# The attention loop's segment mask: made in setup and loaded per group, instead of subtracted by GpSimd

## The reference, cut to what matters

```
edge_dst, edge_src = (edge_index[0], edge_index[1])
...
attn = jnp.einsum('ehd,ehd->eh', q[edge_src], k)
amax = jax.ops.segment_max(attn, edge_src, num_segments=n)
ex = jnp.exp(attn - amax[edge_src])
denom = jax.ops.segment_sum(ex, edge_src, num_segments=n)
alpha = ex / (denom[edge_src] + 1e-16)
upd = jax.ops.segment_sum(v * alpha[..., None], edge_src, num_segments=n)
```

## Time and profile before

| what | us |
|---|---|
| median of 3 runs (5847.3 to 5866.55) | 5865.84 |
| the profiled execution | 5866.98 |
| its span, from the first to the last instruction | 5865.3 |
| stretch of the attention loop in the span | about 1172 to 4355 |
| fourth layer's loop | about 4475 to 5803 |

### The profile page before, as it was taken

The page is one execution under the profiler, slowest core; times in us unless marked ns, Lnnn a source line. Parts: engine busy times, 40 slices in busy tenths (PEclk is TensorE's granted clock), DMA queues, the critical chain, the costliest instruction groups (busy, mean ns, idle before and its releaser), DMA issues. The chain is left out here.

```text
span 5865.3 us, 90896 instructions
## 1 busy us (share of the span) xinstructions
PE 4615.2 (79%) x21193; PEld 3083.9 (53%) x21193; DVE 4524.0 (77%) x9249; ACT 2238.6 (38%) x4760; POOL 3018.0 (51%) x3095
## 2 busy tenths in 40 slices
PE   2888757689999999999999999999975555555556
PEld 1222223256666666666666666666643555555554
DVE  6999863389999999999999999999974443444444
ACT  1777710045555555555555555555531000000001
POOL 0000000066666666666666666666643556556563
PEclk7999969599999999999999999999985555555555
DMA  2121125176666666666666666666622333333332
GB/s 54 74 88 78 75 109 217 30 159 146 139 146 141 145 144 141 146 139 146 143 142 146 139 148 140 141 147 140 145 50 63 79 80 80 79 79 80 79 80 46
DMA packets 524063, 666.30 MB, mean 114 GB/s; under 512 B 187704, under 2 KB 299256, under 8 KB 519928
## 3 DMA queue, kind: packets, MB, share of 16 engines
q1 hardware_dynamic: 469512, 582.29, 40.9%
q0 software_dynamic: 52288, 81.11, 6.3%
q10 hardware_dynamic: 2160, 1.76, 0.1%
HBM read 610.09 MB, written 54.79 MB: 113 GB/s over the span
## 5 line engine op out<-in xcount | busy, mean ns | idle before, releaser
L1506 POOL DMA_INDIRECT msg_rows<-a_rows,msg_idx x808 | 796.1, 985 | 567.3 <-ACT msg_idx L1478 335.7
L1315 DVE TENSOR_TENSOR attn_z<-attn_xt,attn_sh 128x512 f32<-128x512 f32 x1010 | 970.2, 976 | 28.1 <-ACT attn_xt L1036 7.6
L1095 POOL DMA_INDIRECT attn_rows<-x_twice,attn_idx x808 | 874.7, 1083 | 223.3 <-issue 202.4
L1049 ACT CAST attn_z_hi<-attn_z 128x512 fp32r<-128x512 f32 x1010 | 623.0, 620 | 616.7 <-DVE attn_z L1315 492.3
L1544 PE MATMUL msg_at_dst<-msg_bwin,msg_pick 128*128 128x64 f32 x1616 | 397.5, 428 | 572.6 <-DVE msg_pick L1570 509.4
L1113 POOL TENSOR_TENSOR acc_den<-acc_den,attn_sums 128x256 f32 x808 | 628.8, 778 | 189.3 <-POOL acc_den L1113 151.6
L1544 PEld LDWEIGHTS msg_at_dst<-msg_bwin,msg_pick 128*128 128x128 f32 x1616 | 359.9, 328 | 646.3 <-DVE msg_pick L1570 545.7
L1129 POOL TENSOR_TENSOR attn_vx<-attn_ex,attn_vw 128x512 f32<-128x512 f32 x202 | 331.0, 1638 | 588.0 <-ACT attn_ex L1074 588.0
L837 POOL TENSOR_TENSOR x_t<-x_t,ln_rec 64x416 f32<-64x416 f32 x12 | 12.7, 1056 | 1148.3 <-DVE ln_rec L826 1148.3
L1321 DVE TENSOR_TENSOR attn_z_lo<-attn_z,attn_z_hi 128x512 fp32r<-128x512 f32 x808 | 553.8, 685 | 16.8
L1484 ACT ACTIVATE msg_msg<-msg_pre 128x256 f32<-128x256 f32 x202 | 84.1, 417 | 1235.9 <-DVE msg_pre L1585 941.1
(11 more groups left out here) (256 smaller groups left out, 11039.9 us busy)
## 6 DMA issues: line engine op xcount, KB each, us to landing
attn_sh<-in_edge_sh SPq DMA_DIRECT2D x404, 640.0 KB
attn_dst<-dst_scaled SPq DMA_DIRECT2D x202, 256.5 KB
attn_qwin<-q_rows SPq DMA_DIRECT2D x808, 64.0 KB
msg_dst<-dst_scaled SPq DMA_DIRECT2D x202, 256.0 KB
counts<-chunk SPq DMA_DIRECT2D x15, 3100.0 KB, 9.4
chunk_late<-counts SPq DMA_DIRECT2D x15, 3100.0 KB, 10.5
attn_feat<-in_edge_feat SPq DMA_DIRECT2D x202, 128.0 KB
msg_bwin<-b_rows SPq DMA_DIRECT2D x808, 32.0 KB
```

Source lines behind the costliest of these rows:

```text
L1049: nc.scalar.copy(z_hi[p][:, c, :], z[:, c % 2, :]).then_inc(high_sb, 1)
L1095: pool.indirect_dma_start(rows[p][:, t, :], None, dram["x_twice"], bass.IndirectOffsetOnAxis(ap=idx[p][:, t:t + 1], axis=0)).then_inc(rows ...
L1315: dve.tensor_tensor(z[:, c % 2, :], xt[p][:], sh[p][:, c, :], ALU.mult).then_inc(z_ready, 1)
L1506: pool.indirect_dma_start(rows[p][:, t, :], None, dram["a_rows"], bass.IndirectOffsetOnAxis(ap=idx[p][:, t:t + 1], axis=0)).then_inc(rows_ ...
```

## The change

`setup` loads a second line of segment numbers, each the number of the edge before (`dst_line_before`, made on the host by a shift of the index table), subtracts on DVE, scales the difference and writes it to DRAM as `dst_step`. `dst_scaled` loses its first element. In the attention loop POOL's `make_mask` is gone. SP loads each group's 512 mask values, broadcast to 128 partitions (256 KB), behind `dst` and ahead of `qwin`, once the second scan of group g-2 has let go of the buffer. The scans wait for that transfer instead of for POOL.

```
@@ setup, sync @@
-            sp.wait_ge(scaled_done, 2)
-            sp.dma_start(dram["dst_scaled"][1:1 + EP].rearrange("(p t) -> p t", p=P), line_scaled[:]).then_inc(scaled_out, 16)
-            sp.dma_start(dram["dst_scaled"][0:1].rearrange("(p t) -> p t", p=1), before[:]).then_inc(scaled_out, 16)
+            sp.wait_ge(scaled_done, 1)
+            sp.dma_start(dram["dst_scaled"].rearrange("(p t) -> p t", p=P), line_scaled[:]).then_inc(scaled_out, 16)
+            sp.wait_ge(scaled_done, 3)
+            sp.dma_start(dram["dst_step"].rearrange("(p t) -> p t", p=P), line_step[:]).then_inc(scaled_out, 16)
@@ setup, vector @@
-            dve.memset(before[:], -DST_SCALE).then_inc(scaled_done, 1)
+            dve.tensor_tensor(line_step[:], line_prev[:], line_cur[:], ALU.subtract).then_inc(scaled_done, 1)
+            dve.wait_ge(scaled_done, 2)
+            dve.tensor_scalar(line_step[:], line_step[:], DST_SCALE, None, ALU.mult).then_inc(scaled_done, 1)
@@ attention_loop, gpsimd @@
-            def make_mask(g, n, p, first):
-                pool.wait_ge(dst_in[p], 16 * (n + 1))
-                if not first:
-                    pool.wait_ge(topped, g - 1)
-                pool.tensor_tensor(mask[p][:, 0:GE], dst[p][:, 0:GE], dst[p][:, 1:GE + 1], ALU.subtract).then_inc(masked, 1)
...
             with pool.Fori(1, G // 2 - 2) as n:
                 weigh(2 * n, 0)
                 gather(2 * n + 3, n + 1, 1, False)
-                make_mask(2 * n + 2, n + 1, 0, False)
                 add(2 * n - 1, 1)
                 weigh(2 * n + 1, 1)
                 gather(2 * n + 4, n + 2, 0, False)
-                make_mask(2 * n + 3, n + 1, 1, False)
                 add(2 * n, 0)
@@ attention_loop, sync @@
                 if not first:
-                    sp.wait_ge(masked, g - 1)
                     sp.wait_ge(pick_ready, g - 1)
-                sp.dma_start(dst[p][:], dram["dst_scaled"][bass.ds(g * GE, GE + 1)].partition_broadcast(P)
+                sp.dma_start(dst[p][:], dram["dst_scaled"][bass.ds(g * GE, GE)].partition_broadcast(P)
                              ).then_inc(dst_in[p], 16)
+                if not first:
+                    sp.wait_ge(topped, g - 1)
+                sp.dma_start(mask[p][:, 0:GE], dram["dst_step"][bass.ds(g * GE, GE)].partition_broadcast(P)
+                             ).then_inc(mask_in[p], 16)
                 if not first:
                     sp.wait_ge(q_ps, g - 1)
@@ attention_loop, vector, maxima @@
                 dve.wait_ge(attn_ps, g + 1)
-                dve.wait_ge(masked, g + 1)
+                dve.wait_ge(mask_in[p], 16 * (n + 1))
```

More of the change, by code:

```diff
@@ L110, in setup @@
         line_scaled = ph.sb("line_scaled", [P, T])
-        before = ph.sb("before", [1, 1])
+        line_prev = ph.sb("line_prev", [P, T], I32)
+        line_step = ph.sb("line_step", [P, T])
         dst_f = ph.sb("dst_f", [P, T])
@@ L120, in setup @@
             (line_cur[:], dram["dst_line"].rearrange("(p t) -> p t", p=P)),
+            (line_prev[:], dram["dst_line_before"].rearrange("(p t) -> p t", p=P)),
             (sb["x_t"][:], dram["x_t"]),
@@ L945, in attention_loop @@
         dst_in = [ph.sem(f"dst_in{p}") for p in two]
+        mask_in = [ph.sem(f"mask_in{p}") for p in two]
         qwin_in = [ph.sem(f"qwin_in{p}") for p in two]
@@ L957, in attention_loop @@
             ph.sem(n) for n in ("xt_sb", "hid_sb", "w_sb", "ex_sb", "vt_sb", "sum_sb", "high_sb"))
-        masked, vx_ready = ph.sem("masked"), ph.sem("vx_ready")
+        vx_ready = ph.sem("vx_ready")
         added, acc_clear = ph.sem("added"), ph.sem("acc_clear")
@@ L968, in attention_loop @@
         sh = [ph.sb(f"sh{p}", [P, KC, GE]) for p in two]
-        dst = [ph.sb(f"dst{p}", [P, GE + 1]) for p in two]
+        dst = [ph.sb(f"dst{p}", [P, GE]) for p in two]
         qwin = [ph.sb(f"qwin{p}", [P, TG, HD]) for p in two]
@@ L1132, in _ @@
                 gather(p, 0, p, True)
-            make_mask(0, 0, 0, True)
             pool.wait_ge(acc_clear, 1)
             gather(2, 1, 0, False)
-            make_mask(1, 0, 1, True)
             weigh(0, 0)
             gather(3, 1, 1, False)
-            make_mask(2, 1, 0, False)
             weigh(1, 1)
             gather(4, 2, 0, False)
-            make_mask(3, 1, 1, False)
             add(0, 0)
@@ L1154, in _ @@
             gather(G - 1, G // 2 - 1, 1, False)
-            make_mask(G - 2, G // 2 - 1, 0, False)
             add(G - 5, 1)
             weigh(G - 3, 1)
-            make_mask(G - 1, G // 2 - 1, 1, False)
             add(G - 4, 0)
@@ L1301, in make_pick @@
                     dve.wait_ge(q_ps, g)
-                dve.tensor_tensor(pick[:], dst[p][:, 1:GE + 1].rearrange("p (t e) -> p t e", t=TG),
+                dve.tensor_tensor(pick[:], dst[p][:].rearrange("p (t e) -> p t e", t=TG),
                                   sb["node_of_part"][:, bass.ds(TG * g, TG)].unsqueeze(2).to_broadcast([P, TG, P]),
@@ L1521, in load @@
                 sp.dma_start(dst[p][:].rearrange("p t e -> p (t e)"),
-                             dram["dst_scaled"][bass.ds(g * GE + 1, GE)].partition_broadcast(P)).then_inc(dst_in[p], 16)
+                             dram["dst_scaled"][bass.ds(g * GE, GE)].partition_broadcast(P)).then_inc(dst_in[p], 16)
                 if not first:
@@ L1655, in scratch @@
             dram[name] = nc.dram_tensor(name, shape, F32, kind="Internal").ap()
-        scratch("dst_scaled", (EP + 1,))
+        scratch("dst_scaled", (EP,))
+        scratch("dst_step", (EP,))
         scratch("rec_in_kept", (D, NP))
@@ L1744 @@
         "dst_line": dst,
+        "dst_line_before": np.concatenate([dst[:1], dst[:-1]]),
         "edge_feat": np.concatenate([a["edge_attr_64"].T, np.zeros((D, pad), a["edge_attr_64"].dtype)], axis=1),
```

## The result

| | median us | lowest to highest | runs |
|---|---|---|---|
| before | 5865.94 | 5847.3 to 5866.55 | 4 |
| after | 5900.3 | 5896.14 to 5904.75 | 4 |

The changed kernel takes 1.0066 times as long (95% interval 1.0044 to 1.0088). It is 34 us slower, forecast were 39; the interval reaches from 26 to 52 us, so the runs don't tell these two numbers apart. Its profiled execution took 5896.14 us with a span of 5894.4, 29.1 above the span of before. The loss lies in the attention loop: 3166.7 us from its first pick to its last against 3128.2, so 38.5 more.

A forecast was written before the change was run, and what follows sets the result against it. DVE's list, 96% busy in the attention loop, was taken as the bound. Additions +38, loop ends -2 and setup +3 made +39 us on 5866.98, thus 5906, median 5905 us; range 5810 to 5945 us.

The forecast's parts named there:

- DVE is the period, and POOL's slack is worth nothing: Attention loop: DVE, busy 96%, sets the group's 15.71 us; a shorter POOL gains nothing by itself.
- The additions slide forward and meet z, L1321 and L1324: Attention loop: without the mask, POOL's additions start earlier and collide with these DVE operations; mean group 0.20 us longer.
- The term of +38 us: Attention loop: the mean group 0.20 us longer through moved additions, over some 196 groups, +38 us.
- the long group of the working: Attention loop: the group worked through, with long additions of 0.73 us, becomes 0.14 us longer.
- some 196 groups: Attention loop: 196 of the 202 groups were said to follow the worked collision pattern.
- It holds: 0 us: SP's queue: the added mask DMA and wait still let the next loads arrive in time, 13.8 against 16.6 us; 0 us.
- DMA bytes, 0: Attention loop: 256 KB more per group stay hidden, as the DMA engines are busy 0.65 of it; 0 us.
- Setup, +3 us: Setup: two more DVE operations, a DMA waited for and 404 KB more to load, +3 us with two mask transfers.
- Ends of the loop, -2 us: First and last groups of the loop: one z or L1324 stretch saved at each end, -2 us.
- The median: Whole kernel: the summed 5906 us, less 1.1 for the median, gave 5905 us.
- z wins the race: Rival, attention loop: first addition comes behind the fifth z, mean group 0.25 us shorter, -49 us, 5818 us; chance 0.13.
- The loads come too late: Rival, attention loop: loads grow beyond some 12.5 us, so every pick waits; about 6060 us for one us; chance 0.10.

The follow-up runs named there:

- e2: Kernel before with the mask removed altogether: POOL does not make it, nothing loads it, the scans read a tile of zeros; 5891.37 us, ratio 1.0043.
- e1: Changed kernel plus a useless POOL subtraction of the mask's size where the mask was made; 5874.77 us, ratio 1.0014.
- e3: Changed kernel plus a write-only POOL memset between the last gather and the column multiplication, so the additions start later; 5848.45 us, ratio 0.997.
- e4: Changed kernel with group g-2's mask loaded in group g's load, so SP does not wait for the running group's scan; 5895.93 us, ratio 1.0045.
- e6: Kernel before, mask on POOL, its column multiplication and additions waiting for DVE's last z remainder of the running group; another chip, 5597.97 us, ratio 1.0058.
- e5: e4's kernel with POOL's column multiplication and additions waiting for DVE's last z remainder of the running group; another chip, 5496.27 us, ratio 0.9873.

## Why the prediction was right, point by point

- **DVE is the period, and POOL's slack is worth nothing.** Right: 288 us less on POOL, and the kernel is slower.
- **The additions slide forward and meet z, L1321 and L1324.** Right, row by row, and shown by e2 (taken away, nothing added), by e1 (put back) and by e3 (moved). Forecast were about 1.1 for z, 1.1 for the fourth L1321 and 1.23 for L1349; measured were 1.14, 1.17 and 1.22 to 1.23 in regular groups. The first addition starts 8.26 us behind the pick, forecast 8.24. L1114 took 0.21 and stands right behind the gather.
- **The term of +38 us.** Of the pattern it speaks of, the size is nearly right too: 0.20 forecast for the mean group, 0.178 measured in e2's regular ones and 0.176 in e4's (0.196 in after's, with SP's order on top), and 0.14 for the long group of the working, which measured 0.15. Mis-sized is in the main the count, "some 196 groups": seven late groups gain 1.0 each instead of losing 0.2. By e2, which has no other effect, the whole term is 26 us (197 groups by 0.133). The earlier trace rows had shown such a group, and the prediction used it for the race alone, without asking how many there were and what they would do.
- **"It holds: 0 us", for SP's order.** This step failed, by about 14 us: after's group is 0.073 longer than e4's, which differs in SP's order alone. That it cancels the miss of 12 above is luck, and the sum came out nearer than its terms. The step asked whether `sh` and `dst` come in time for DVE, and they did, but for one pick near the loop's end. It took the gathers only as something that slows the load. The load slows the gathers as well, and PE waits for those; that way round wasn't weighed. e4 shows that the order and not the bytes did it.
- **DMA bytes, 0.** Right, by e4.
- **Setup, +3 us.** Right. The subtraction and the scaling took 1.00 and 0.58, tables began 2.6 later, and the loop's first pick came at 1185.62 instead of 1183.62. That start spreads by itself: it lies between 1181.7 and 1183.6 in the three profiles with the old setup (before, e2, e6), and between 1183.9 and 1186.5 in the six with the new one, 3.0 apart in the mean.

```profile
29.20 1.00 DVE L203 TENSOR_TENSOR setup_line_step<-setup_line_prev,setup_line_cur 128x808 f32<-128x808 int32 x1
30.23 0.58 DVE L205 TENSOR_SCALAR setup_line_step<-setup_line_step 128x808 f32<-128x808 f32 x1
```

- **Ends of the loop, -2 us.** The savings came: in the first group L1324 took 1.76 before and 0.69 after, in the third z 1.13 and 0.68, and the two z behind the last pick together 3.12 and 2.28, so 2.4 in all. The loop didn't end earlier by them, for the last two groups before the last pick had 4.3 us of idle time, up to 2.98 at one u. They have none in e4, so this belongs to SP's order.
- **The median.** After these terms (26 by the additions' pattern, 14 by SP's order, 3 or so by setup, -2 at the ends) stand 41 us, and the medians lie 34 apart. In the profiles the fourth layer's loop is 9 us shorter after, which I put to its spread; why the medians lie 7 us closer than the terms is not shown.
- **Rivals.** "z wins the race" happened in the seven late groups alone. In all others the first addition is recorded ahead of z, by 0.08 to 0.22 us in the regular ones. In 15 of the 21 groups with idle time the fifth z is short too (under 0.8), but not by winning: DVE's waits had put it 0.47 to 3.8 us behind that addition, which was over, or nearly so, when z began. The rival was priced too low, 0.25 where e3 measured 0.45: the prediction let L1108 run clean and the first addition wait for z, while in e3 L1108 is the one that waits, and the additions behind it keep their old places. "The loads come too late" happened in a mild form, at the gathers instead of at `dst`.

What stays open: why just 22 groups had idle time on DVE when PE waited 171 times, why POOL is late in one group of 28, and what in the fourth layer's loop takes 300 us more on one chip than on the other.

## What to carry to other kernels

Where two engines shut each other out, an operation taken from the one with slack changes when its next ones run, so lay both timelines side by side and move everything behind the removed one forward before counting a gain. Count how many stretches follow the pattern that you work out, and price the others by themselves. A wait put into the queue that feeds all loads delays the largest of them too, and the one who pays can be another queue's transfer that it now meets; give such a load the place where its condition has long been met.

## What the runs showed of the hardware

- The exclusion holds for the smallest operation: DVE's L1361 of 128x1 took 0.67 in the mean instead of 0.21 (e5), as much more as a z of 128x512 loses to the mask. What a collision costs hung on how long the other still ran: L1361 began 0.58 before the addition's end and lost 0.37 (e5's row), z 0.57 before the mask's end and lost 0.44, and the scan L1349 0.61 before the addition's end and lost 0.45.
- The recorded starts don't tell who goes first. In the earlier trace rows a mask recorded 0.18 behind z went first and z took 1.78. In the late group of after L1114 is recorded 0.18 behind z as well (2497.62, 2497.44), and z went first. In e3 L1116 is recorded 0.01 ahead of z (2509.57, 2509.58), took 0.74 instead of 0.20, and z kept its 0.68. The Trainium skill ("SBUF — State Buffer", section "Who interferes with whom") gives the ports to the one that issues first; issue itself isn't in these rows, so they neither bear it out nor refute it, and a race with a margin under some 0.2 us can't be called from a trace.
- A burst of plain loads slows gathers that are under way: with `sh` issued in the middle of them their packets took 7.2% of the DMA engines' time in the span and PE waited 162 us for rows in the loop; with `sh` behind them, at the same bytes, it was 6.4% and PE didn't wait for rows at all (e4).
